# Softmax attention: the reciprocal of the packed sums moved from VectorE to ScalarE, as the exponential of the negative logarithm

## The reference, cut to what matters

```python
x = x + jnp.tanh(g_xattn[0]) * _L0_xattn_ref(_layernorm(x, axis=-1), ctx_2048, Wq, bq, Wk, bk, Wv, bv, Wo, bo)
...
scores = jnp.einsum('bhtc,bhsc->bhts', q, k) / math.sqrt(K_CH)
p_attn = jax.nn.softmax(scores, axis=-1)
out = jnp.einsum('bhts,bhsc->bhtc', p_attn, v)
out = out.transpose(0, 1, 3, 2).reshape(b, N_HEADS * K_CH, t_t)
return _proj(out, Wo, bo)
```

## Time and profile before

| | us |
|---|---|
| median of 3 runs | 2579.21 |
| lowest, highest | 2570.91, 2582.12 |
| the profiled execution's own time | 2583.23 |
| its span, first to last instruction | 2581.4 |
| TensorE busy in it | 2209.2 (86%) |
| VectorE busy | 1835.6 (71%) |
| ScalarE busy | 1153.9 (45%) |
| POOL busy | 1106.4 (43%) |

### The profile page before, as it was taken

The page is one execution under the profiler, slowest core; times in us unless marked ns, Lnnn a source line. Parts: engine busy times, 40 slices in busy tenths (PEclk is TensorE's granted clock), DMA queues, the critical chain, the costliest instruction groups (busy, mean ns, idle before and its releaser), DMA issues. The chain is left out here.

```text
span 2581.4 us, 60448 instructions
## 1 busy us (share of the span) xinstructions
PE 2209.2 (86%) x20880; PEld 1675.0 (65%) x20880; DVE 1835.6 (71%) x3965; ACT 1153.9 (45%) x2509; POOL 1106.4 (43%) x1111
## 2 busy tenths in 40 slices
PE   6899888887678899994899998999988599999990
PEld 4555555543666677762677777777776477888880
DVE  4888888873546688765878878878787374545754
ACT  2776767665434333323444444444333264333330
POOL 3455554466144221002555445455487600334736
PEclk9988988886799999996999999999989799999995
DMA  5455554452359333312332332322334372445855
GB/s 114 120 124 137 147 136 129 104 144 85 120 171 296 110 107 120 92 58 53 82 89 57 83 84 60 85 73 69 81 96 116 129 253 82 136 141 182 264 172 148
DMA packets 250723, 313.10 MB, mean 121 GB/s; under 512 B 45248, under 2 KB 202944, under 8 KB 250432
## 3 DMA queue, kind: packets, MB, share of 16 engines
q1 hardware_dynamic: 189456, 219.11, 30.5%
q0 software_dynamic: 26624, 58.79, 8.3%
q10 hardware_dynamic: 34352, 31.34, 3.6%
HBM read 122.40 MB, written 102.24 MB: 87 GB/s over the span
## 5 line engine op out<-in xcount | busy, mean ns | idle before, releaser
L2136 POOL TENSOR_TENSOR ca_qk<-ca_qk,ca_q_swap 128x512 f32<-128x512 f32 x160 | 249.2, 1557 | 365.7 <-DVE ca_q_swap L2314 365.3
L735 DVE TENSOR_REDUCE soft_top<-soft_pa 128x2 fp32r<-128x512 f32 x512 | 327.9, 682 | 90.4 <-PE soft_pa L816 87.9
L630 ACT ACTIVATE soft_prob<-soft_pb 128x512 f32<-128x512 f32 x512 | 286.1, 594 | 180.9 <-PE soft_pb L809 179.1
L809 PE MATMUL soft_pb<-soft_rep 32*128 32x256 f32 x1024 | 207.5, 359 | 58.0 <-DVE soft_top L735 30.9
L809 PEld LDWEIGHTS soft_pb<-soft_rep 32*128 32x128 f32 x1024 | 135.0, 211 | 175.6 <-issue 81.3
L816 PE MATMUL soft_pa<-soft_rep 31*128 31x256 f32 x1024 | 217.4, 366 | 6.0 <-DVE soft_top L735 3.5
L1469 PE MATMUL moe_py<-moe_w_d,moe_at 128*128 x788 | 214.2, 387 | 1.5 <-issue 1.1
L1450 PE MATMUL moe_pgu<-moe_w_hi,moe_xt_hi 128*128 x472 | 192.9, 409 | 24.1 <-DVE moe_xt_lo L1362 13.4
L2406 PE MATMUL ca_py<-ca_w_hi,ca_ot_hi 128*128 128x256 f32 x512 | 155.8, 304 | 37.9 <-DVE ca_ot_lo L2335 37.8
L1368 DVE TENSOR_TENSOR moe_act_f<-moe_silu,moe_pgu 128x256 f32<-128x256 f32 (+1 forms) x236 | 88.6, 375 | 133.7 <-ACT moe_silu L1263 129.7
L2314 DVE TENSOR_TENSOR ca_q_swap<-ca_q_swap,ca_sin_q 128x512 f32<-128x512 f32 x128 | 116.8, 913 | 82.3 <-DMA ca_q_swap<-ca_q_f 81.9
(11 more groups left out here) (377 smaller groups left out, 6265.7 us busy)
## 6 DMA issues: line engine op xcount, KB each, us to landing
ca_q_swap<-ca_q_f SPq DMA_DIRECT2D x640, 64.0 KB
moe_xs<-moe_rows SPq DMA_DIRECT2D x236, 128.0 KB, 2.1
soft_rep<-soft_parts SPq DMA_DIRECT2D x378, 64.0 KB
moe_rows<-soft_blank SPq DMA_DIRECT2D x27, 768.0 KB
moe_ys_rows<-moe_ys ACTq DMA_DIRECT2D x134, 128.0 KB
moe_ys<-moe_ys ACTq DMA_DIRECT2D x102, 128.0 KB
moe_xd<-scratch SPq DMA_DIRECT2D x64, 128.0 KB, 2.5
ca_vs<-ca_v SPq DMA_DIRECT2D x32, 256.0 KB, 3.9
```

The lines of the kernel that those rows point to most:

```text
L630: act.activation(prob[:, k % 4, h, :], p_b[:, 2 * T * h:2 * T * (h + 1)], ACT.Exp).then_inc(prob_ready, 1)
L735: dve.tensor_reduce(heads[:, j, :, g], p_a[:, 2 * T * h:2 * T * (h + 1)].rearrange("p (c s) -> p c s", c=HALF), AX, ALU.max).then_inc(a_do ...
L809: mm = pe.matmul(p_b[:, out], rep[of, i % 4, g, at:at + PART], rep[of, i % 4, g, 0:T], start=True, stop=True)
L2136: pool.tensor_tensor(qk[:, u % 2, m, :], qk[:, u % 2, m, :], q_swap[:, p % 2, :], ALU.add).then_inc(qk_ready, 1)
```

## The change

VectorE's reciprocal is taken out. On ScalarE, in iteration i, Ln of the sums of tile i-1 is written into `rsum` between `exp(i, 6)` / `keep(i, 1)` and `exp(i, 7)`, behind the same waits that the reciprocal had; behind `exp(i, 7)` an Exp with scale -1 turns it into the reciprocal, in place, and raises `rsum_ready`. One semaphore is new.

```diff
+        log_ready = sem("log")
...
                     exp(i, 6)
                     keep(i, 1)
+                    t = i - 1
+                    if live(t):
+                        act.wait_ge(pack_in[t % 2], PACK * (t // 2 + 1))
+                        past(act, on_ready, t)
+                        act.activation(rsum[:], sums[:, t % 2, :], ACT.Ln).then_inc(log_ready, 1)
                     exp(i, 7)
+                    if live(t):
+                        act.wait_ge(log_ready, t + 1)
+                        act.activation(rsum[:], rsum[:], ACT.Exp, scale=-1.0).then_inc(rsum_ready, 1)
                     if routed(i - 4):
                         route.scale(act, i - 4, lambda t: xo[:, t % KEEP, :])
...
                     if i == RANK + 3:
                         route.weigh(dve)
-                    t = i - 1
-                    if live(t):
-                        dve.wait_ge(pack_in[t % 2], PACK * (t // 2 + 1))
-                        past(dve, on_ready, t)
-                        dve.reciprocal(rsum[:], sums[:, t % 2, :]).then_inc(rsum_ready, 1)
```

## The result

The change makes the kernel slower: 2655.2 us median (2652.2 to 2666.8, 4 runs) against 2579.9 us (2570.9 to 2582.1, 4 runs), a ratio of 1.0313 over all runs, 95% interval 1.0282 to 1.0345 (the medians alone lie 75.3 us apart, 1.0292). The profiled execution took 2652.2 us with a span of 2650.4, 69.0 more than before. The forecast was 2677 with a range of 2600 to 2745: the direction held, and so did the mechanism (two loads a tile, paid at the tile's end); the size was 75 us where 98 were forecast. A profile shows one execution, and executions of one kernel lie 15 to 25 us apart here, 0.5 to 0.8 us a tile, so a tile's time and clock from a profile are less certain than a ratio.

The account below looks back on a forecast made before the run. No engine is full; TensorE, VectorE and ScalarE are coupled, ScalarE setting the pace at the tile boundary. The profiled 2583.2 us plus 79 (2.5 a tile) and 19 for the clock gives 2681, less 4: 2677, range 2600 to 2745.

Parts of the forecast that it names:

- Two loads a tile: On ScalarE, Ln between exponentials forces two table loads a tile, 64 of 1.28 us, 82 us in all.
- Rival 1: No table loads in the attention stage, Ln and Exp sharing one table: 25 us more, 2604 us; chance 0.13.
- Before exponential 7: ScalarE at the tile's end: load, wait for sums, Ln and load delay exponential 7 by 3.3 us.
- the load behind the wait: Ahead of Ln on ScalarE: if the load follows the wait for sums, that wait is 1.0 to 1.6 us.
- What TensorE gets back: At the tile boundary, present TensorE waits for maxima and the peak's transfer not lost twice: 1.2 us a tile, at most 1.4.
- up by over 60 us: Sign that the forecast is right: TensorE's waits for ScalarE grow by over 60 us.
- The clock: Attention stage: more standing lowers the granted clock, time at 1.2 GHz rising from 24% to 35%, costing 19 us.
- Rival 3: The clock falls for most of the attention stage: 132 us on top of the 79, 2790 us; chance 0.10.
- VectorE's relief: Removing 55.9 us of VectorE reciprocals is worth at most TensorE's 24.2 us of waits for maxima, 0.86 us a tile.
- The steps after it keep their length: Steps behind the tile boundary stay as long, set by TensorE and VectorE; ScalarE's room there does not help.
- The lower bound of 1.8 us a tile: Least net loss at the boundary, with all 1.4 us given back and sums never late; 2.5 was forecast.
- Rival 2: Faster: ScalarE absorbs the added 0.78 us a tile and VectorE's 24 us of wait returns, 2555 us; chance 0.04.

Follow-up runs that it names:

- shared table: The changed kernel with one preload, behind the gate's Tanh, of a table holding both Ln and Exp: ratio 1.0068, 2591.0 us.
- four loads a tile: The kernel before, reciprocal kept, with unused one-column Ln, Exp, Ln added ahead of exponential 7: ratio 1.0654, 2740.6 us.
- removal alone: The kernel before without VectorE's reciprocal and nothing in its place; POOL multiplies by the sums instead: ratio 0.9948, 2559.3 us.
- loads alone: The kernel before, reciprocal kept, with an unused one-column Ln ahead of exponential 7, adding two table loads a tile: ratio 1.0317, 2656.8 us.
- the pair behind `y`: The changed kernel with the Ln/Exp table preloaded and Ln and Exp side by side behind `y`: ratio 0.9921, 2554.3 us.
- mid tile: The changed kernel, still two table loads a tile, with Ln and Exp behind exponential 2 for tile i-2: ratio 1.0244, 2637.7 us.

## Why the prediction was right, and where its sizes were off

**Two loads a tile**: 64 counted, 1283 ns each, as taken from the lone exponential among Silus. Each adds no more than its own length: at 376.37 to 379.39 load, Ln, load and exponential follow each other within 0.02 us. By the Trainium skill (ScalarE: Activation LUTs, What ACT_TABLE_LOAD costs) each switch would have had a drain besides, 88 us in all (an estimate from its 1.38 us each); this trace has none. Rival 1 was wrong for the change as written. Its price was near: the shared table, asked for by hand, costs 0.68%, some 18 us, where 25 were worked out. What the Trainium skill says (ScalarE: Activation LUTs, Table sets: the hidden batching unit), that one set holds both functions, is borne out by that run; this program had it loaded only with the line that asks for it.

**Before exponential 7**, 3.3 us forecast (1.30 + 0.3 + 0.39 + 1.30), 3.14 measured. Ln took 0.416 us, not 0.39; the wait for the sums beyond the load was 4.8/28 = 0.17 us, not 0.3. Its other bound, the load behind the wait, did not come: the load runs first, as the wait for the sums shows, 4.8 us with the loads and 38.9 without. With Exp 3.56 us against 3.7.

**What TensorE gets back**, 1.2 us a tile, was right in its own two terms: its waits for maxima and for the peaks' transfer fell by 15.6 and 15.7 us, 1.1 us a tile. The term that was mis-sized is the one beside it. The forecast counted all 3.7 us that ScalarE is late as standing of TensorE, and put nothing for what TensorE does in that time, though it names it (step 7 and values 2). The new waits are 52.4 us ahead of step 0, 25.7 more for `y` and 1.4 for exponentials, 79.5 us or 2.8 us a tile; the sign "up by over 60 us" is met only with the row that the profile gives no releaser. Before the change step 0 came 1.65 us behind the first half of exponential 7, now 0.10: exponential 7 could be 1.55 us late there without cost, in part for the transfer's wait already counted, in part for TensorE's own work. By the windows TensorE is idle for 100.8 us of the changed stretch against 58.0, 1.5 us a tile more, where 2.5 were forecast.

**The clock** fell from 0.88 to 0.81 (24% to 38% of the stretch at 1.2 GHz; 35% was forecast). TensorE is busy for 468.3 us against 443.5 with the same 4146 matmuls, 0.9 us a tile more, where the forecast had 19/31 = 0.6. These 0.9 and the 1.5 above are the 2.41 us by which the tile grew, against 3.1 forecast. It is an account of TensorE's time and not yet of causes: a slow matmul can lie where TensorE would have waited, and no run holds the clock fixed. At the 0.3 us of the earlier trace rows the 3.4 us more at the lower level would be 1.0 us a tile. Two neighbouring tiles above, 22.8 us at 0.80 and 20.0 at 0.84, differ in their work as well (169 and 154 matmul rows). Rival 3, the clock low for most of the stage, did not come, not even with four loads a tile (0.76).

**VectorE's relief.** Alone, the removal gives 0.56 us a tile by the profiles (17.91 - 17.35) and 0.4 by the ratio. In the changed kernel it seems worth more: with the reciprocal kept, 2.74 us of delay cost 2.66, with it removed 3.56 cost 2.41, 1.07 us more returned. By the ratios it is some 0.85, with intervals of 0.3 on either side of each cost, and the stretches say where it lies:

| us, mean of 28 tiles | end of 6 to exponential 0 | exponential 0 to end of 6 | tile | clock |
|---|---|---|---|---|
| before | 3.60 | 14.31 | 17.91 | 0.88 |
| removal alone | 3.71 | 13.64 | 17.35 | 0.89 |
| loads alone | 5.52 | 15.05 | 20.57 | 0.78 |
| changed | 6.13 | 14.19 | 20.32 | 0.81 |
| shared table | 4.75 | 13.47 | 18.22 | 0.86 |

The removal acts in the steps behind exponential 0 (14.31 to 13.64 without loads, 15.05 to 14.19 with them) and not at the tile's end. The lower clock of the loads alone is a rival for part of the second difference, and was not separated. "The steps after it keep their length" held as a number, 14.19 us against 14.31, but as two things that cancel: the relief shortens them, and the loads, with the clock that falls behind them, lengthen them (14.31 to 15.05).

**Small slips.** The lower bound of 1.8 us a tile comes out as 2.0 from its own terms, and two loads and two activations (3.4 us) in place of 1.75 are 1.65 us, not about 1. The first lifts the lower bound by some 6 us, the second the forecast by 0.7.

**Rival 2**, ScalarE absorbs the work, failed by the place, as its own condition said: TensorE's wait for `y` went from 4.0 to 29.7 us. It had counted only 0.78 us of work on ScalarE, which holds only without the loads. With the shared table and the pair behind `y` the kernel did become faster, 0.9921. That the time, 2554.3 us, is the rival's 2555 is partly luck: it was measured on a chip where the kernel before took 2575.3, and of the 24.2 us of waits for maxima, which were its price, 15.7 are still there.

## What to carry to other kernels

An engine's share of busy time does not say what it can take: look at where its idle time lies in its own order, and put new work there, behind what others wait for and after its operands have landed. With one table, the same two activations in place of the reciprocal cost 0.7% ahead of exponential 7 and gained 0.8% behind `y`; with a load ahead of each the order was the reverse, 3.1% and 4.3%, so a place has to be tried with what really stands in it. Before using a second table function inside a run of exponentials, look for a set that holds both and load it by hand once: 1.3 us a switch, twice a tile, was nearly four fifths of the loss here. A block on an engine in a coupled pipeline is covered by the gap that it stands in and by the work that its neighbours still have beside it; what goes beyond is paid, however much the engine idles elsewhere. Here 2.7 us at the tile's end cost 2.6, the next 3.0 cost 2.8, and 3.4 us in mid tile about 2.5 (against the removal alone).

## What the runs showed of the hardware that was not expected

A power with a 128x256 operand takes 41.3 us on POOL, 57 times its product of the same shape (0.73 us), while a 128x1 power took 0.56 us in the kernel before. From these two sizes it is 0.16 us for each element of a partition (an estimate; no other size was run). In these runs a table load did not wait with its activation: it ran ahead of the wait for the sums, and the wait is 1.39 us a tile without loads and 0.17 with them.
